# Turning the rows of h and y with a DMA transpose instead of with TensorE, in a two-layer graph kernel

## The chip, the core and the metric

The kernel runs on one core of a Trainium2 chip. The metric is the device time of one execution in microseconds (us). The engines work side by side, each on its own in-order list of instructions, and wait for each other by semaphores: TensorE (PE, with its weight loads shown apart as PEld), VectorE (DVE), ScalarE (ACT), GpSimd (POOL), and SyncE (SP), which here issues every DMA.

## What is computed

Shapes: `x` is 3125 x 256, there are 50,000 edges (`src`, `dst`), all weights are 256 wide.

```python
vals = 1 / deg(src)                                  # per row of the sum
def layer(x, W, b):                                  # used twice: W0, b0 and W1, b1
    neigh = segment_sum(vals * x[dst], src)
    return relu(concat([x, neigh]) @ W.T + b)
x = layernorm(x + layer(layer(x, W0, b0), W1, b1))
h_sparse = maxk(x @ W_neigh, 32)                     # only the 32 largest of each row stay
x = layernorm(x + x @ W_self + segment_sum(h_sparse[src], dst) / max(deg(dst), 1))
```

## The kernel before

The 3125 rows are cut into NT = 25 tiles of P = 125. First (up to about 183 us) the kernel builds the 25 x 25 blocks of the edge count matrix in SBUF (`ct`, `region[T]`), and stores a second copy of it in DRAM (`c_dram`) for the last part. A sum over neighbours is then a product with that matrix. All operands are float16 pairs, a high part and a low part side by side (`xs`, `a1`, `part`: 2 x 256 columns), so that one pass carries both.

**Layer 0** (`aggregate(0, T, ..)`, L1550 to L1560): 25 matmuls of 512 columns, one for each source tile ("blocks" below), sum tile T into one of three PSUM banks. DVE adds the halves, scaled, to `own_in` (`first_half` L901, `second_half` L906). ACT writes the high part of h, a relu, into `part[T % 2]` (`h_high` L1211), DVE the low part (L919). Then the 125 rows of `part` must be turned, because the next product wants the features on the partitions. PE does it with four matmuls against the identity into a PSUM bank (`turn` L1459 to L1462, called by `turn_h`), and ACT copies that to `tr_sb` (`tr_out` L1198 to L1202). `product(T)` (L1573) then multiplies `tr_sb` with the weights in six matmuls (`in_parts` L1455). ACT takes its two halves out (`own1_out` L1213: `own_st`, which SP stores, and the high part of `a1`), DVE makes the low part (`a1_low` L909).

Between these, DVE sums the count matrix of tile T + 2 (`sum_tree` L809) for the degrees, PE finishes them with two small matmuls (`degrees` L1584) and DVE inverts them (`invert` L888). ACT sums the other direction (`degree` L1221).

**Layer 1** does the same with `a1`: t2, then x is added and the rows normalised (L968 to L986), ACT writes the high part of y into `part` (L1277), POOL the low part (`y_low` L545), PE turns it (`turn_y`), `product(NT + T)` follows, and ACT takes out `hn` and `z_st` (`dense_out`). DVE picks the 32 largest of `hn` three tiles later (L936 to L953).

**The last part** is another 625 blocks (`last_sum` L1674), with the matrix loaded back from DRAM (`load_c` L408), and the second layernorm.

The order on every engine is written out by hand:

- PE, layer 0 (L1628 to L1654): from T = 5 on, 17 blocks of tile T, `turn_h(T - 1)`, 8 blocks, `degrees(T + 1)`, `product(T - 1)`. So a product runs one tile behind its sum.
- PE, crossing from layer 0 to 1 (L1657 to L1666): the blocks of tiles 0 and 1 of layer 1 are mixed with the turn and the product of the last tile, and with the waits for `a1_lo`.
- PE, layer 1 (L1667 to L1671): 12 blocks of tile T, `turn_y(T - 2)`, 13 blocks, `product(NT + T - 2)`.
- SP, layer 0 (L397 to L401): `load_own(0, T + 2)` (L375, waits for t2 of the tile before), `store_own1(T - 1)` (L385).
- SP, crossing (L418 to L429): two loads of x, the bias, `load_own(1, 0)` and `(1, 1)`, the last store, the weights.
- SP, layer 1 (L430 to L438): `load_own`, `load_x`, `store_z(T - 2)`, a wait for the sum of tile T, and `load_c(T - 1)` (763 KB).

Of the kernel before, what the change touches and what calls it, by code (L numbers as in the profile page):

```python
# [84 lines left out]
def gnn(nc, x, src, dst, w0, b0, w1, b1, wself, wneigh, out):  # L85
    ctx = ExitStack()
    with ctx:
# [131 lines left out]
        part = [lay(f"part{i}", [P, 2 * F], F16) for i in range(2)]  # L219
# [38 lines left out]
        tp = [bank[i][:, 0:4 * P].rearrange("p (c n) -> p c n", c=4) for i in (5, 6, 7)]  # L258
# [23 lines left out]
        slab_ready, tr_zeroed, eye_added, deg_summed = sem("slab_ready"), sem("tr_zeroed"), sem("eye_added"), sem("deg_summed")  # L282
# [14 lines left out]
        tp_done, tp_copied, mm_done = sem("tp_done"), sem("tp_copied"), sem("mm_done")  # L297
# [28 lines left out]
        def _(sp):  # L326
# [97 lines left out]
            load_bias(1, b1)  # L424
            load_own(1, 0)
# [35 lines left out]
        def _(pool):  # L461
# [71 lines left out]
            for t in tr_sb:  # L533
                nc.gpsimd.memset(t[:, :, P:128], 0.0).then_inc(tr_zeroed, 1)
# [7 lines left out]
            def y_low(T):  # L542
                pool.wait_ge(y_high, T + 1)
                out = part[T % 2]
# [21 lines left out]
        def _(dve):  # L566
# [348 lines left out]
            for T in range(NT):  # L915
# [3 lines left out]
                v.scalar_tensor_tensor(part[T % 2][:, F:2 * F], t2[T % 2][:, :], 0.0, part[T % 2][:, 0:F],  # L919
# [5 lines left out]
                if T:  # L925
                    a1_low(T - 1)
# [84 lines left out]
        def _(act):  # L1011
# [186 lines left out]
            def tr_out(i):  # L1198
                act.wait_ge(tp_done, i + 1)
                if i > 1:  # L1200
                    act.wait_ge(mm_done, i - 1)
                a.activation(tr_sb[i % 2][:, :, 0:P], tp[i % 2], ACT.Copy).then_inc(tp_copied, 1)  # L1202

            def part_free(i):
                if i > 1:
                    act.wait_ge(tp_done, i - 1)

            def h_high(T):
                act.wait_ge(t2_ready, T + 1)
                part_free(T)  # L1210
                a.activation(part[T % 2][:, 0:F], t2[T % 2][:, :], ACT.Relu).then_inc(hi_ready, 1)  # L1211
# [26 lines left out]
            for T in range(NT):  # L1238
                if T + 1 < NT:
                    degree(T + 1, 0)  # L1240
                if T == 1:
                    act.wait_ge(tr_zeroed, 2)
                if T:
                    tr_out(T - 1)
                if T == 0:
                    h_high(0)
# [7 lines left out]
                if T:  # L1254
                    own1_out(T - 1)
            tr_out(NT - 1)
# [17 lines left out]
            def y_high_part(T):  # L1274
                act.wait_ge(normed, T + 1)
                part_free(NT + T)
                a.activation(part[T % 2][:, 0:F], t2[(NT + T) % 2][:, :], ACT.Copy).then_inc(y_high, 1)  # L1277
# [5 lines left out]
            for T in range(NT):  # L1283
                if T > 1:
                    tr_out(NT + T - 2)
# [5 lines left out]
            tr_out(2 * NT - 2)  # L1291
            dense_out(NT - 2)
            sp_high_part(NT - 3)
            tr_out(2 * NT - 1)
# [10 lines left out]
        def _(pe):  # L1305
# [153 lines left out]
            def turn(out, parts, done):  # L1459
                for c in range(4):  # L1460
                    last = mm(out[:, c, :], parts[:, c * 128:(c + 1) * 128], ident16[:, 0:P], start=True, stop=True)  # L1461
                last.then_inc(done, 1)  # L1462

# [98 lines left out]
            def turn_h(T):  # L1562
                pe.wait_ge(lo_ready, T + 1)
                if T > 1:
                    pe.wait_ge(tp_copied, T - 1)
                turn(tp[T % 2], part[T % 2], tp_done)

            def turn_y(T):
                pe.wait_ge(y_ready, T + 1)
                pe.wait_ge(tp_copied, NT + T - 1)  # L1570
                turn(tp[(NT + T) % 2], part[T % 2], tp_done)

            def product(i):  # L1573

                pe.wait_ge(tp_copied, i + 1)
# [58 lines left out]
            aggregate(0, 3, 0, 9)  # L1634
            product(1)
            aggregate(0, 3, 9, 17)
            degrees(3)
            aggregate(0, 3, 17, NT)
            turn_h(2)
            aggregate(0, 4, 0, 9)  # L1640
            product(2)
            degrees(4)
            aggregate(0, 4, 9, 20)
            turn_h(3)
            aggregate(0, 4, 20, NT)
            degrees(5)
            product(3)
# [9 lines left out]
            pe.wait_ge(a1_lo, NT - 2)  # L1657
            aggregate(1, 0, 0, 11)
            turn_h(NT - 1)
            aggregate(1, 0, 11, 17)  # L1660
            product(NT - 1)
            aggregate(1, 0, 17, NT - 2)
            aggregate(1, 1, 0, 12)
            pe.wait_ge(a1_lo, NT)
            aggregate(1, 0, NT - 2, NT)
            aggregate(1, 1, 12, NT)  # L1666
# [23 lines left out]
            turn_y(NT - 2)  # L1690
# [3 lines left out]
            turn_y(NT - 1)  # L1694
# [5 lines left out]
            pe.wait_ge(tp_copied, 2 * NT)  # L1700
# [33 lines left out]
```

## Time and profile before

| what | value |
|---|---|
| time, three runs | 676.26, 677.28 and 681.02 us; median 677.28 us |
| the profiled execution | span 680.0 us from its first to its last instruction, on the one core; no other time of it is listed |
| mean granted TensorE clock | 0.984 of full speed |
| DMA | 73.09 MB, 107 GB/s on the average of the span |

The span of the profiled execution lies between the three times, 2.7 us above their median. Times in the rows below are microseconds from the span's start; a row of the timeline gives start, duration, engine, line, operation, output<-input, and in brackets how long the engine had been idle and what ended that. Layer 0 runs from about 183 to 363 us, layer 1 to 536 us, the last part to the end.

### The profile page before, as it was taken

The numbers are of one execution on the slowest core, as the hardware profiler recorded it, in microseconds if no ns is written. First come the engines' busy times: TensorE is split into PE (matmuls) and PEld (weight loads), VectorE is DVE, ScalarE is ACT, GpSimd is POOL, SyncE is SP. The second block draws the span as 40 slices with busy tenths as digits, with TensorE's granted clock in tenths as the row PEclk, the third lists the DMA queues.
The fourth block names the chain that finished last, engine by engine and source line by source line (L and its number), as shares of the span: only waits on it lengthen the run. The fifth ranks groups of instructions, "written<-read, shape, count | busy, mean of one in ns | idle before, by whom it ended". The sixth has DMA issues, their size and how long they took to land.

```text
span 680.0 us, 11272 instructions
## 1 busy us (share of the span) xinstructions
PE 650.4 (96%) x3982; PEld 337.4 (50%) x3983; DVE 496.9 (73%) x1274; ACT 338.8 (50%) x654; POOL 108.6 (16%) x187
## 2 busy tenths in 40 slices
PE   8788899999988999999999999999999999999996
PEld 3466566676534444444444444444444444444442
DVE  8898969999768788787882587878878855643333
ACT  3768779999768576767673233333333320000000
POOL 3001122222111001010110323222232210000000
PEclk9898979999999899999999999999999999999999
DMA  8643635555521111111112556565656423310000
GB/s 205 116 130 108 214 120 167 171 167 167 158 67 46 31 37 40 33 44 31 46 32 69 158 159 186 153 190 152 180 163 178 137 80 115 116 31 24 25 28 23
DMA packets 39543, 73.09 MB, mean 107 GB/s; under 512 B 3120, under 2 KB 32207, under 8 KB 39481
## 3 DMA queue, kind: packets, MB, share of 16 engines
q1 hardware_dynamic: 39481, 72.30, 35.8%
q8 instruction: 34, 0.56, 0.4%
q14 instruction: 28, 0.23, 0.1%
HBM read 38.91 MB, written 33.38 MB: 106 GB/s over the span
## 4 chain that ended last, share of the span: by engine, by line
PE 81%; DVE 10%; ACT 3%; DMA 2%; issue 2%; SPq 0%; POOL 0%; DVEq 0%; POOLq 0%; ACTq 0%
PE pair L1557 34%; PE bank L1681 10%; PE pair L1681 10%; PE bank L1481 6%; PE bank L1455 5%; PE bank L1447 4%; PE pair L1455 4%; PE pair L1367 4%; DVE hots L637 2%; PE bank L1461 1%; DVE tree L820 1%; DMA own_in<-own_dram 1%; DMA wparts_dram<-w_parts 1%; PE pair L1346 1%; PE bank L1467 1%
## 5 line engine op out<-in xcount | busy, mean ns | idle before, releaser
L1557 PE MATMUL pair<-xs,ct 125*128 125x512 f16 x625 | 143.7, 380 | 0.0
L1557 PE MATMUL pair<-a,ct 125*128 125x512 f16 x625 | 142.8, 379 | 0.0
L637 DVE TENSOR_TENSOR hots<-iota,jobs 125x1792 f16<-125x1792 f16 (+1 forms) x100 | 103.1, 1064 | 5.0 <-PE pair L1367 4.4
L1557 PEld LDWEIGHTS pair<-a,ct 125*128 125x128 f16 x625 | 61.1, 99 | 68.1
L1557 PEld LDWEIGHTS pair<-xs,ct 125*128 125x128 f16 x625 | 60.9, 100 | 67.6 <-issue 1.4
L1068 ACT ACTIVATE slab<-pair 125x875 f16<-125x875 f32 (+1 forms) x100 | 83.3, 854 | 13.2 <-PE pair L1367 8.6
L1226 ACT ACTIVATE a<-ct 125x1000 f16<-125x1000 f16 (+1 forms) x75 | 80.2, 1069 | 8.2 <-DMA c_dram<-slab 7.3
L1681 PE MATMUL bank<-xs,ct 125*128 125x512 f16 (+1 forms) x325 | 71.5, 379 | 0.0
L1681 PE MATMUL pair<-xs,ct 125*128 125x512 f16 x300 | 66.4, 379 | 0.0
L529 POOL TENSOR_TENSOR own_in<-own_in,bias_sb 125x256 f32<-125x256 f32 x50 | 38.2, 765 | 168.3 <-DMA own_in<-own_dram 168.2
L1301 ACT ACTIVATE sd<-mv,epsb 125x1 f32<-125x1 f32 x25 | 7.4, 294 | 113.9 <-DVE mv L1004 113.9
L1447 PEld LDWEIGHTS bank<-ident,slab 125*128 125x128 f16 x625 | 41.2, 100 | 39.8 <-issue 26.5
L901 DVE SCALAR_TENSOR_TENSOR t<-pair,rdeg,own_in 125x256 f32<-125x256 f32 x50 | 24.1, 483 | 50.3 <-PE pair L1557 46.9
L1447 PE MATMUL bank<-ident,slab 125*128 125x125 f16 x625 | 52.4, 223 | 6.3 <-DVE ct L791 3.0
L1367 PE MATMUL pair<-hots 125*128 125x125 f16 x625 | 52.8, 224 | 5.6 <-DVE hots L637 4.6
L1481 PE MATMUL bank<-w_t,x_t 128*125 128x512 f32 x100 | 56.0, 643 | 1.1 <-ACT x_t L1111 1.1
L1681 PEld LDWEIGHTS bank<-xs,ct 125*128 125x128 f16 (+1 forms) x325 | 32.3, 100 | 37.8
L1202 ACT ACTIVATE tr_sb<-bank 128x500 f16<-128x500 f32 x50 | 29.1, 581 | 42.3 <-PE bank L1461 42.3
L1367 PEld LDWEIGHTS pair<-hots 125*128 125x128 f16 x625 | 41.1, 100 | 11.6 <-issue 9.4
L1681 PEld LDWEIGHTS pair<-xs,ct 125*128 125x128 f16 x300 | 29.8, 99 | 34.4
L791 DVE COPY ct<-bank 125x1008 f16<-125x1008 f16 x50 | 33.6, 673 | 13.8 <-PE bank L1447 13.8
L820 DVE TENSOR_TENSOR tree<-tree,ct 125x630 uint16<-125x630 uint16 x75 | 37.3, 497 | 2.6
(205 smaller groups left out, 829.7 us busy)
## 6 DMA issues: line engine op xcount, KB each, us to landing
c_dram<-slab SPq DMA_DIRECT2D x25, 683.6 KB
ct<-c_dram SPq DMA_DIRECT2D x25, 683.6 KB
own_in<-own_dram SPq DMA_DIRECT2D x50, 125.0 KB
own_dram<-own SPq DMA_DIRECT2D x25, 125.0 KB
own_dram<-own_st SPq DMA_DIRECT2D x25, 125.0 KB
x_in<-in_x_dram SPq DMA_DIRECT2D x25, 125.0 KB
z_dram<-z_st SPq DMA_DIRECT2D x25, 125.0 KB
a<-z_dram SPq DMA_DIRECT2D x5, 625.0 KB
```

The costliest lines, as they stand in the source:

```text
L529: nc.gpsimd.tensor_tensor(own_in[k % 2][:, :], own_in[k % 2][:, :], bias_sb[:, :], ALU.add).then_inc(own_biased, 1)
L637: v.tensor_tensor(hots[k][:, :, :, :].rearrange("p w g (a d) -> p (w g) a d", d=2), iota, job, ALU.is_equal).then_inc(win_hot, 1)
L791: v.tensor_copy(ct[:, TG0[g]:TG0[g] + TG[g], t, :], tr16[1][0:P, 0:TG[g], 0:PC]).then_inc(tr_free[1], 1)
L820: step(v.tensor_tensor(tree[:, :], tree[:, :], quint[k], ALU.add))
L1068: a.activation(slab3[t % 2][:, :, lo * QW:hi * QW].rearrange("p b (w d) -> p b w d", d=QW), pair[f % 2][0:P, 0:n, 0:QKEY].rearrange("p w ( ...
L1226: a.activation(unread[:, 0:(hi - lo) * P].rearrange("p (b s) -> p b s", s=P), ct[:, lo:hi, T, 0:P], ACT.Copy, accum_out=deg_part[:, T, k:k ...
L1367: last = mm(pair[f % 2][:, u, 0:QKEY], hots[f][:, u, 0, :], hots[f][:, u, 1, 1:QKEY + 1], start=True, stop=True, skip_group_check=True)
L1447: last = nc.tensor.transpose(tr16[g % 2][:, i, 0:P], slab[par][:, (TG0[g] + i) * P:(TG0[g] + i) * P + 128], ident16[:, 0:P])
L1455: last = mm(out, lhs(2 * pt + h), w[:, h, q, :], start=h == 0 and k == 0, stop=h == 1 and k == 2, skip_group_check=True)
L1481: last = mm(bank[6][0:P, :].rearrange("p (a f) -> p a f", a=2), x_t32[:, h, :], w0_t[:, h::2, :], start=h == 0, stop=h == 1, skip_group_ch ...
L1557: ins = mm(agg[k % 3][0:lhs.shape[1], :], lhs, parts[l][:, t, :], start=t == 0, stop=t == NT - 1, skip_group_check=True)
L1681: ins = mm(out3[T % 8][0:lhs.shape[1], :], lhs, xs[:, b, :], start=b == 0, stop=b == NT - 1, skip_group_check=True)
```

## The change

The four turning matmuls, the bank they wrote and the ACT copy go. SP issues one DMA for each tile instead, `turn(i)`, which moves `part[i % 2]` (now 128 x 512, the lowest rows zeroed once) transposed to `tr_sb[i % 2]`. `product(i)` waits for that DMA (`turned`), and ACT waits for it before it overwrites `part`. To give the DMA room, in layer 0 every `product`, `own1_out`, `a1_low` and `store_own1` comes one tile later than before; in layer 1 the products keep their places. The zeroing of the padding moves from `tr_sb` to `part` and behind a wait.

```diff
+            def turn(i):                                      # on SP
+                sp.wait_ge(y_ready if i >= NT else lo_ready, i % NT + 1)
+                if i > 1:
+                    sp.wait_ge(mm_done, i - 1)
+                sp.dma_start_transpose(tr_sb[i % 2][:, :, :], part[i % 2][:, :]).then_inc(turned[i % 2], 16)
...
             for T in range(NT):                               # SP, layer 0
                 if T + 2 < NT:
                     load_own(0, T + 2)
-                if T:
-                    store_own1(T - 1)
+                turn(T)
+                if T > 1:
+                    store_own1(T - 2)
...
             load_bias(1, b1)                                  # SP, crossing
+            store_own1(NT - 2)
             load_own(1, 0)
...
             for T in range(NT):                               # SP, layer 1
+                if T:
+                    turn(NT + T - 1)
                 if T + 2 < NT:
                     load_own(1, T + 2)
...
+            turn(2 * NT - 1)
             store_z(NT - 2)
...
-            for t in tr_sb:                                   # POOL
-                nc.gpsimd.memset(t[:, :, P:128], 0.0).then_inc(tr_zeroed, 1)
+            pool.wait_ge(a0_split, NT + 2)
+            for i, t in enumerate(part):
+                nc.gpsimd.memset(t[96:128, :], 0.0).then_inc(part_zeroed, 1)
+                pool.wait_ge(part_zeroed, i + 1)
...
-                if T:                                         # DVE, layer 0; ACT's own1_out likewise
-                    a1_low(T - 1)
+                if T > 1:
+                    a1_low(T - 2)
+            a1_low(NT - 2)
             a1_low(NT - 1)
...
-            def tr_out(i):                                    # ACT; its calls go too
-                act.wait_ge(tp_done, i + 1)
-                if i > 1:
-                    act.wait_ge(mm_done, i - 1)
-                a.activation(tr_sb[i % 2][:, :, 0:P], tp[i % 2], ACT.Copy).then_inc(tp_copied, 1)
             def part_free(i):
                 if i > 1:
-                    act.wait_ge(tp_done, i - 1)
+                    act.wait_ge(turned[i % 2], 16 * (i // 2))
...
             def product(i):                                   # PE
-                pe.wait_ge(tp_copied, i + 1)
+                pe.wait_ge(turned[i % 2], 16 * (i // 2 + 1))
...
-            turn_h(0)                                         # PE, layer 0
             aggregate(0, 2, 9, 20)
-            product(0)
             degrees(2)
             aggregate(0, 2, 20, NT)
-            turn_h(1)
...
-            for T in range(5, NT):
-                aggregate(0, T, 0, 17)
-                turn_h(T - 1)
+            product(0)
+            for T in range(3, NT):
+                aggregate(0, T, 0, 8)
+                product(T - 2)
+                aggregate(0, T, 8, 17)
+                if T < 5:
+                    degrees(T)
                 aggregate(0, T, 17, NT)
-                if T + 1 < NT:
+                if 4 < T + 1 < NT:
                     degrees(T + 1)
-                product(T - 1)
...
+            pe.wait_ge(a1_lo, NT - 3)                         # PE, crossing
+            aggregate(1, 0, 0, 8)
+            product(NT - 2)
+            aggregate(1, 0, 8, NT - 3)
+            aggregate(1, 1, 0, 8)
             product(NT - 1)
+            pe.wait_ge(a1_lo, NT - 1)
+            aggregate(1, 0, NT - 3, NT - 1)
+            aggregate(1, 1, 8, NT - 1)
             pe.wait_ge(a1_lo, NT)
+            aggregate(1, 0, NT - 1, NT)
+            aggregate(1, 1, NT - 1, NT)
             for T in range(2, NT):                            # PE, layer 1
-                aggregate(1, T, 0, 12)
-                turn_y(T - 2)
-                aggregate(1, T, 12, NT)
+                aggregate(1, T, 0, NT)
                 product(NT + T - 2)
```

In the last part the two remaining turns (`turn_y(NT - 2)`, `turn_y(NT - 1)`) and the wait for the last copy go in the same way.

## Rows read from the trace of the kernel before

**Rows 1.** The page, part 4: shares of the chain that ended last, by engine.

```profile
PE 81%; DVE 10%; ACT 3%; DMA 2%; issue 2%; SPq 0%; POOL 0%; DVEq 0%; POOLq 0%; ACTq 0%
```

**Rows 2.** Busy time in stretches: length, busy us (instructions) of each engine, PEclk, DMA.

```profile
222.00:363.00 141.00, 141.00 (x737) 68.17 (x736) 110.21 (x311) 96.82 (x194) 14.54 (x19) 0.99 0.12 36
...
383.00:536.00 153.00, 153.00 (x775) 71.27 (x774) 119.47 (x430) 51.75 (x131) 42.94 (x65) 1.00 0.58 170
```

**Rows 3.** The chain in order of time, one tile of each layer: start, us, what.

```profile
301.60 3.67 PE pair L1557 x17
305.49 1.73 PE pair L1557 x8
307.28 1.32 PE bank L1455 x6
...
431.38 1.30 PE pair L1455 x6
432.68 2.59 PE pair L1557 x12
435.50 2.81 PE pair L1557 x13
```

**Rows 4.** Groups of instructions by line, the turning matmuls (busy us, mean ns | idle).

```profile
L1461 PE MATMUL bank<-ident,part 125*128 125x125 f16 x200 | 19.2, 218 | 1.7 <-issue 1.3 <-POOL part L545 0.4
```

**Rows 5.** The timeline, one tile of layer 0, from t2 to the low part of a1.

```profile
300.36 0.48 DVE L901 SCALAR_TENSOR_TENSOR t<-pair,rdeg,own_in 125x256 f32<-125x256 f32 x1 [0.48 <-PE pair L1557]
...
301.39 0.25 SPq L383 DMA_DIRECT2D own_in<-own_dram  x1
...
301.84 0.43 DVE L919 SCALAR_TENSOR_TENSOR part<-t,part 125x256 f16<-125x256 f32 x1 [0.48 <-ACT part L1211]
...
304.96 0.73 POOL L529 TENSOR_TENSOR own_in<-own_in,bias_sb 125x256 f32<-125x256 f32 x1 [6.30 <-DMA own_in<-own_dram]
...
306.43 0.48 DVE L911 SCALAR_TENSOR_TENSOR a<-pair,unscale,a 125x256 f16<-125x256 f32 x1
```

**Rows 6.** The timeline, one tile of layer 1, from t2 to the low part of y.

```profile
431.53 0.49 DVE L901 SCALAR_TENSOR_TENSOR t<-pair,rdeg,own_in 125x256 f32<-125x256 f32 x1 [1.32 <-PE pair L1557]
...
434.24 0.74 SPq L412 DMA_DIRECT2D ct<-c_dram  x2
...
437.33 0.67 POOL L545 TENSOR_TENSOR part<-t,part 125x256 f16<-125x256 f32 x1 [4.92 <-ACT part L1277]
```

**Rows 7.** The timeline, the first tiles of layer 0.

```profile
203.82 0.42 DVE L919 SCALAR_TENSOR_TENSOR part<-t,part 125x256 f16<-125x256 f32 x1 [0.81 <-ACT part L1211]
...
210.59 0.15 DVE L891 TENSOR_SCALAR rdeg<-bank 125x1 f32<-125x1 f32 x1
...
217.01 0.15 DVE L891 TENSOR_SCALAR rdeg<-bank 125x1 f32<-125x1 f32 x1
...
221.36 0.22 PE L1589 MATMUL bank<-ones,deg 125*125 125x1 f16 x1 [2.45 <-DVE deg L827]
```

**Rows 8.** Busy time in one of the stretches of 1 us behind that wait.

```profile
222.00:223.00 1.00, 1.00 (x3) 0.29 (x2) 0.58 (x2) 0.35 (x1) 0.00 (x0) 0.50 0.00 0
```

**Rows 9.** The chain in order of time: behind that wait, and the crossing between the layers.

```profile
221.64 2.43 PE bank L1455 x6
224.07 4.24 PE pair L1557 x17
...
363.18 1.31 PE bank L1455 x6
366.75 7.63 DMA own_in<-own_dram
...
382.98 1.30 PE bank L1455 x6
```

**Rows 10.** The timeline of the crossing: t2 and y of the first tile of layer 1.

```profile
375.33 0.48 DVE L901 SCALAR_TENSOR_TENSOR t<-pair,rdeg,own_in 125x256 f32<-125x256 f32 x1 [3.29 <-POOL own_in L529]
...
379.05 0.67 POOL L545 TENSOR_TENSOR part<-t,part 125x256 f16<-125x256 f32 x1 [2.79 <-ACT part L1277]
```

More of the change, by code:

```diff
@@ L218, in gnn @@
         t2 = [lay(f"t2_{i}", [P, F], F32) for i in range(2)]
-        part = [lay(f"part{i}", [P, 2 * F], F16) for i in range(2)]
+        part = [lay(f"part{i}", [128, 2 * F], F16) for i in range(2)]
         tr_sb = [lay(f"tr_sb{i}", [128, 4, 128], F16) for i in range(2)]
@@ L257, in gnn @@
         xp = bank[7][:, 0:2 * P].rearrange("p (c n) -> p c n", c=2)
-        tp = [bank[i][:, 0:4 * P].rearrange("p (c n) -> p c n", c=4) for i in (5, 6, 7)]
         agg, dense = bank[0:3], bank[3:5]
@@ L281, in gnn @@
         win_hot, win_done, win_read = sem("win_hot"), sem("win_done"), sem("win_read")
-        slab_ready, tr_zeroed, eye_added, deg_summed = sem("slab_ready"), sem("tr_zeroed"), sem("eye_added"), sem("deg_summed")
+        slab_ready, part_zeroed, eye_added, deg_summed = sem("slab_ready"), sem("part_zeroed"), sem("eye_added"), sem("deg_summed")
         tr_cleared = sem("tr_cleared")
@@ L296, in gnn @@
         hi_ready, lo_ready = sem("hi_ready"), sem("lo_ready")
-        tp_done, tp_copied, mm_done = sem("tp_done"), sem("tp_copied"), sem("mm_done")
+        turned, mm_done = [sem("turned0"), sem("turned1")], sem("mm_done")
         own1_copied, own1_stored, a1_hi, a1_lo = sem("own1_copied"), sem("own1_stored"), sem("a1_hi"), sem("a1_lo")
@@ L543, in y_low @@
                 pool.wait_ge(y_high, T + 1)
-                out = part[T % 2]
+                out = part[(NT + T) % 2][0:P, :]
                 nc.gpsimd.tensor_tensor(out[:, F:2 * F], t2[(NT + T) % 2][:, :], out[:, 0:F], ALU.subtract).then_inc(y_ready, 1)
@@ L918, in _ @@
                 dve.wait_ge(hi_ready, T + 1)
-                v.scalar_tensor_tensor(part[T % 2][:, F:2 * F], t2[T % 2][:, :], 0.0, part[T % 2][:, 0:F],
+                v.scalar_tensor_tensor(part[T % 2][0:P, F:2 * F], t2[T % 2][:, :], 0.0, part[T % 2][0:P, 0:F],
                                        ALU.max, ALU.subtract).then_inc(lo_ready, 1)
@@ L1210, in h_high @@
                 part_free(T)
-                a.activation(part[T % 2][:, 0:F], t2[T % 2][:, :], ACT.Relu).then_inc(hi_ready, 1)
+                a.activation(part[T % 2][0:P, 0:F], t2[T % 2][:, :], ACT.Relu).then_inc(hi_ready, 1)
             def own1_out(T):
@@ L1240, in _ @@
                     degree(T + 1, 0)
[L1241 to L1244, printed above, removed]
                 if T == 0:
+                    act.wait_ge(part_zeroed, 2)
                     h_high(0)
@@ L1253, in _ @@
                     act.wait_ge(deg_summed, NT * len(DG))
-                if T:
-                    own1_out(T - 1)
-            tr_out(NT - 1)
+                if T > 1:
+                    own1_out(T - 2)
+            own1_out(NT - 2)
             own1_out(NT - 1)
@@ L1276, in y_high_part @@
                 part_free(NT + T)
-                a.activation(part[T % 2][:, 0:F], t2[(NT + T) % 2][:, :], ACT.Copy).then_inc(y_high, 1)
+                a.activation(part[(NT + T) % 2][0:P, 0:F], t2[(NT + T) % 2][:, :], ACT.Copy).then_inc(y_high, 1)
             def sp_high_part(T):
@@ L1284, in _ @@
                 if T > 1:
-                    tr_out(NT + T - 2)
                     dense_out(T - 2)
@@ L1290, in _ @@
                     sp_high_part(T - 3)
-            tr_out(2 * NT - 2)
             dense_out(NT - 2)
             sp_high_part(NT - 3)
-            tr_out(2 * NT - 1)
             dense_out(NT - 1)
@@ L1457, in in_parts @@
                 return last
[L1459 to L1462, printed above, removed]
             def own_transposes(t, rows_):
@@ L1560, in aggregate @@
                     ins.then_inc(agg_done, 1)
[L1562 to L1571, printed above, removed]
             def product(i):
-                pe.wait_ge(tp_copied, i + 1)
+                pe.wait_ge(turned[i % 2], 16 * (i // 2 + 1))
                 if 1 < i < NT + 2:
@@ L1689, in _ @@
             last_sum(0, 0, 20)
-            turn_y(NT - 2)
             last_sum(1, 0, 8)
@@ L1693, in _ @@
             last_sum(1, 8, 20)
-            turn_y(NT - 1)
             pe.wait_ge(t2_ready, 2 * NT)
@@ L1699, in _ @@
             last_sum(3, 0, 20)
-            pe.wait_ge(tp_copied, 2 * NT)
             last_sum(4, 0, 20)
```

22 lines of the change are left out of this document (removed).

## Prediction

> **What bounds the kernel now.** I began with the shares of the chain that ended last: PE is 81% of it and ACT, where the removed copy ran, 3% [rows 1]. That is an average, so the next view is busy time by stage: through most of layer 0 and all of layer 1 PE is busy without a gap, 141.00 of 141.00 us and 153.00 of 153.00 us, while DVE has 110 and 119, ACT 97 and 52 [rows 2]. In these stages PE's work alone sets the pace, and what PE no longer does is gained as long as nothing makes it wait. The chain in order of time then gives the pace of a tile [rows 3]. Layer 0: 17 blocks 3.67 us, a gap to the next piece of 305.49 - 305.27 = 0.22 us, 8 blocks 1.73, degrees 0.06, product 1.32: 7.00 us. Layer 1: 1.30 + 2.59 + 0.23 + 2.81 = 6.93 us. A block is 3.67 / 17 = 0.216 us.
>
> The gap is the turn. Its rows have a mean of 218 ns for 200 matmuls and 19.2 us busy [rows 4], and the reader could take 19.2 us for the price. But matmuls overlap, so their durations hold latency that the next one covers. What a turn takes from the pace is the 0.22 us.
>
> **The change part by part.**
>
> *Removed on PE.* Fifty turns of 0.22 us are 11.0 us, 1.6% of the span, and this is the most the change can bring. ACT's 50 copies go too; ACT is off the chain in both layers, so they are worth nothing.
>
> *Does another engine become the bound?* Without the turn, PE's tile is 6.78 us in layer 0 and 6.70 in layer 1. DVE's own tile in layer 0 runs from 300.36 to 306.43 + 0.48 = 306.91, so 6.55 us with the idle 0.48 before it left out [rows 5]. It stays under 6.78, by only 0.23 us. In layer 1 DVE sits idle 1.32 us of every 6.9 [rows 6], which leaves 5.6. PE stays the bound and keeps the whole 0.22.
>
> *Added: one transposing DMA for each tile.* Call D the time from the moment its input is ready to the moment PE may start the product. No row shows such a DMA, nor any from SBUF to SBUF. The nearest row by size (125 KB against 128 KB) is the load of `own_in`: issued at 301.39, used by POOL at 304.96, 3.57 us [rows 5]. The longest of its kind, with other loads ahead of it in the queue, took 7.63 us [rows 9]. From below the bound is the issue alone, 0.25 us [rows 5]. I take 3.5 us, next to the nearest row, for in layer 0 the DMA engines are 12% busy [rows 2] and little lies ahead in the queue.
>
> *What hides D.* Layer 0: the sum of a tile ends 307.28 - 7.00 - 0.06 = 300.22, its low part at 301.84 + 0.43 = 302.27, 2.05 us later [rows 3, 5]. Its product now comes a whole tile and 8 blocks behind, 6.78 + 0.06 + 1.73 = 8.57 us after that sum. Cover: 6.5 us. Layer 1: the sum ends at 431.38, POOL ends y at 438.00, 6.62 us later [rows 3, 6]; the product stands two tiles behind, 13.40 us. Cover: 6.8 us. The 763 KB of `load_c`, issued at 434.24, go ahead in the same queue and have 3.8 us until then [rows 6]; the engines are 58% busy [rows 2], so most of that has passed. With D = 3.5 both steady states lose nothing.
>
> *What queues behind the new waits on SP.* In layer 0 it is `store_own1`, which has more than a tile's time. In layer 1 it is `load_own`, `load_x`, `store_z` and `load_c`; the turn is issued 6.62 us after a sum, and the next of these waits for t2 of the following tile, about 8.0 us after. So SP loses nothing if the issue takes up to 1.4 us; an issue here takes 0.25 [rows 5]. If it takes longer, `load_own` comes later, and it is used a tile afterwards.
>
> *The first tiles of layer 0.* Here DVE sets the pace: its `invert` of tiles 3 and 4 are 6.42 us apart, and PE sits idle 2.45 us at `degrees(5)` [rows 7]. The four turns saved up to there are worth nothing. Worse, PE has `product(1)` ahead of `degrees(3)`, on which DVE waits. The low part of tile 1 is ready at 204.24 [rows 7]; + 3.5 is 207.74; + product 1.30 + 9 blocks 1.94 is 210.98, so `invert(3)` starts some 0.5 us behind its 210.59. PE reaches `degrees(4)` another 25 blocks and a product later, 6.70 us, at 217.7, 0.8 us behind 217.01. That passes on to `degrees(5)`: +0.8 us.
>
> *Layer 0 from tile 5.* Twenty turns (4 to 23) at 0.22: -4.4 us.
>
> *The crossing.* Count from the end of the last sum of layer 0, now 363.18, called A. PE's new order: 8 blocks, product, 22 blocks, product, 18 blocks, 2 blocks: 50 x 0.216 + 2 x 1.32 = 13.44 us until both first sums of layer 1 are done, then 25 blocks to `product(NT)` at A + 18.8. `load_own(1, 0)` is now issued 3.57 us after A and lands 7.63 later [rows 9]. In the new order it follows a store that waits for product 23, at some A + 4.0, so its bias is added by about A + 12.4. In time. So t2 starts at A + 13.4, y follows 379.72 - 375.33 = 4.39 later [rows 10], at A + 17.8, plus D is A + 21.3. PE waits 2.5 us for the first turned y, with nothing else it may do. Today that product starts at 382.98 - 363.18 = 19.8 [rows 9], so the crossing gets 1.5 us longer though it holds two turns less.
>
> *What that wait costs besides.* After the idle 2.45 us at 221.36 [rows 7] the granted clock was 0.50, the lower level of 1.2 GHz [rows 8], and the next product took 2.43 us and the next 17 blocks 4.24, against 1.32 and 3.67 at 2.4 GHz [rows 3, 9]: 1.7 us lost. A wait of 2.5 us is the same size, so I add 1.7.
>
> *Layer 1 and after.* Twenty-four turns (y 1 to 24): -5.3 us. The last y has more than the 6.8 us of cover, since 20 blocks of the last part come in between.
>
> *At nothing.* POOL's larger memsets and their wait lie in a stretch in which POOL then waits for the bias. With that cover gone they would cost their own length, under 1 us, once. `a1_low` and `own1_out` are moved by a tile, not added.
>
> **The sum.** 0.8 - 4.4 + 1.5 + 1.7 - 5.3 = -5.7 us on the span of 680.0, which is -0.84%. On the median of 677.28 that is 671.6 us. In D the sum moves by 2 us for each us: once in the first tiles, once in the crossing.
>
> **The rivals.**
>
> *A quicker DMA, nearly the whole gain.* With D = 2.5 the first tiles lose nothing and the crossing waits 1.5 us. Waits of that size are not among the rows that show a fall of the clock, so the 1.7 goes: -4.4 + 0.5 - 5.3 = -9.2, 668.1 us. For it: both ends are in SBUF, and a round trip to DRAM, which the 3.57 us hold, falls away. Against it: turning is more than copying, and no row shows its speed.
>
> *A middling DMA, nearly nothing gained.* With D = 5.5, about the middle between 3.57 and 7.63, the sum is -5.7 + 2 x 2.0 = -1.7, 675.6 us. The mechanism is that the four groups of 128 columns are turned one behind the other, while each copying row above is one stream. The Trainium skill ("VectorE: DVE Perf Modes", section on the three transpose paths) speaks against the change here: it gives 1309 ns for a 128 x 128 block by DMA and 390 ns on TensorE. Four blocks in a row would by that page be an estimated 5.2 us, and the sum -2.3. For TensorE the trace disagrees with it in this place: four blocks take 0.22 us from the pace [rows 3].
>
> *Slower: the DMA outlasts its cover.* Up to D = 6.4 the sum stays below zero. Beyond 6.5 PE waits at every product of layer 0, and its tile becomes 2.05 + D - 1.79 = D + 0.26. At D = 7.0 that is 7.26 instead of 7.00: 20 x 0.26 = +5.2; first tiles 0.8 + 3.5 = 4.3; crossing 1.5 + 3.5 + 1.7 = 6.7; layer 1 at (6.62 + 7.0) / 2 = 6.81 instead of 6.93: -2.9. Sum +13.3, 690.5 us. For it: such waits have been 7.63 us here [rows 9]. Against: only with other loads ahead.
>
> *The change does nothing to the pace.* If DVE's tile in layer 0 grows by the 0.23 us that it has left, layer 0 keeps 6.99 and its 4.4 us are lost; the sum is -1.3, 676.0. The four engines' in-order waits were read from one tile, so this can't be excluded.
>
> **How the numbers follow.** Chances: forecast 0.40, quicker 0.24, middling 0.13, slower 0.18, DVE in the way 0.05. A change of 1% (6.8 us) is about what a measurement of this kernel tells from none. The quicker case lies beyond it, and of the forecast's own spread, 669 to 674.5 us (D from 3.0 without the fall of the clock to 5.0), some quarter does: faster 0.34. Slower by over 1% is the slower case: 0.18. The rest, 0.48, is within 1%. The range is 667.0 to 684.0: below, the quicker case with a little to spare; above, the slower case up to D of some 6.6, which leaves about 0.15 of the chance out there.
>
> **What would show it.** Right: the chain has 7.00 -> 6.78 and 6.93 -> 6.70 us for a tile, PE waits for `turned` at `product(NT)` alone, some 2.5 us, with a granted clock of 0.50 behind it, and `degrees(3)` comes later than now. Wrong: PE waits before every product (D above 6.5), DVE without idle time before t2 in layer 0, or the rows of SP showing an issue of several us, which would move `load_c` and `load_own` too. The single number that decides is D.

## The result, and the profile after

The changed kernel takes 692.96 us (median of 4 runs, 692.39 to 699.1) against 679.15 us for the kernel before (4 runs). The quotient of these two medians is 1.0203; the ratio on record, which isn't formed from them, is 1.0237, with a 95% interval of 1.0178 to 1.0295. So it is slower; the interval leaves open whether by more than 2%. The forecast was 671.6 us and its range ended at 684.0. The profiled execution took 692.39 us, with a span of 690.6 us.

First the page, part 4, of the changed kernel: shares of the chain that ended last, by engine and (first entries) by line. It answers to [rows 1].

```profile
PE 58%; DMA 17%; DVE 11%; SPq 6%; ACT 5%; issue 3%; POOL 0%; DVEq 0%; ACTq 0%
```

PE fell from 81% to 58%; the DMA, 2% before, has 17%, and SP's own queue 6%. Next the busy time in the two layers, as in [rows 2].

```profile
222.00:357.00 135.00, 135.00 (x656) 63.24 (x655) 108.97 (x306) 85.23 (x171) 14.36 (x19) 1.00 0.26 57
383.00:545.00 162.00, 145.36 (x657) 63.20 (x655) 116.13 (x420) 38.98 (x105) 42.52 (x63) 1.00 1.16 169
```

In layer 0 PE is still busy without a gap. In layer 1 it is idle for 16.6 of 162 us, and the DMA's share went from 0.58 to 1.16 although it moves the same 169 GB/s (170 before). A share above 1 can't be work: transfers that wait are counted as busy.

The chain in order of time gives the tile of layer 0, to set beside [rows 3]:

```profile
295.32 1.75 PE pair L1554 x8
297.07 1.30 PE pair L1457 x6
298.37 3.67 PE pair L1554 x17
302.04 0.00 PE bank L1575
302.04 0.06 PE bank L1576
```

From 295.32 to 302.10 it is 6.78 us, as forecast. In layer 1 the chain no longer runs on PE. One round of it:

```profile
413.89 8.56 DMA tr_sb<-part
...
422.49 1.48 PE bank L1457 x6
...
424.00 0.47 ACT hn L1269
424.47 0.37 ACT z_st L1272
...
424.86 1.03 SPq L423
...
426.00 1.32 SPq L419
...
427.37 1.19 SPq L419
...
428.65 8.88 DMA tr_sb<-part
```

This is a closed loop through SP's in-order list: the turn lands, the product runs, ACT takes it out, SP stores z (L423), issues the two parts of `load_c` (L419), and only then issues the turn of the tile after next. A round takes 428.65 - 413.89 = 14.76 us for two tiles. PE's timeline over one of these tiles shows what is left for it:

```profile
414.98 1.47 PE L1457 MATMUL pair<-w_lay,tr_sb 128*128 128x512 f16 x6 [1.07 <-DMA tr_sb<-part]
416.28 5.56 PE L1554 MATMUL pair<-a,ct 125*128 125x512 f16 x25
422.49 1.47 PE L1457 MATMUL bank<-w_lay,tr_sb 128*128 128x512 f16 x6 [0.65 <-DMA tr_sb<-part]
```

Before every product PE waits for the turn, and a tile is 422.49 - 414.98 = 7.51 us (median of the layer 7.59) instead of 6.91. The turn's own rows, in layer 0 and then in layer 1 (duration is the issue on SP; below it the time from issue to landing):

```profile
L389 SPq DMA_TRANSPOSE tr_sb<-part x25: 1189/1191/1298, 193.5 to 358.3; - x25
DMA to landing us min/median/max: 2.4/3.0/4.4
...
L389 SPq DMA_TRANSPOSE tr_sb<-part x25: 1194/1278/2172, 374.9 to 551.7; - x25
DMA to landing us min/median/max: 2.4/9.0/10.0
```

The same transfer takes 3.0 us in one layer and 9.0 in the other. By stages, each measured from the first matmul named to the next (degrees(T) is the pair of small matmuls; the build of the count matrix ends where the first block of layer 0 starts):

| stage | before, us | after, us | difference | forecast |
|---|---|---|---|---|
| build of the count matrix | 183.46 | 179.11 | -4.4 | 0 |
| first block to degrees(5) | 37.91 | 39.69 | +1.8 | +0.8 |
| degrees(5) to degrees(24) | 134.66 | 130.51 | -4.2 | -4.4 |
| degrees(24) to the first product of layer 1 | 26.79 | 28.08 | +1.3 | +1.5, and +1.7 for the clock |
| from there to the first block of the last part | 153.42 | 169.76 | +16.3 | -4.8 (22 turns) |
| the rest | 143.77 | 143.41 | -0.4 | -0.4 (2 turns) |

The build is not touched by the change; in the profiles below it lies between 179.1 and 183.7 us without any order, so it is left out of every comparison. The other five rows add up to +14.8 us, near the 13.8 between the two medians; the forecast's own sum was -5.7. One stage holds the whole surprise.

### The profile page after: what moved, and what is told of

Its sections match the earlier page's. It is cut to its first block, busy times and chain, and to the rows that moved or that the text cites. A ratio compares the mean times of both kernels' runs of the same rounds, so it can differ in the third digit from the quotient of the medians.

```text
span 690.6 us, 10824 instructions
## 1 busy us (share of the span) xinstructions
PE 639.2 (93%) x3782; PEld 323.4 (47%) x3783; DVE 498.3 (72%) x1274; ACT 314.0 (45%) x604; POOL 110.7 (16%) x187
## 4 chain that ended last, share of the span: by engine, by line
PE 58%; DMA 17%; DVE 11%; SPq 6%; ACT 5%; issue 3%; POOL 0%; DVEq 0%; ACTq 0%
PE pair L1554 17%; DMA tr_sb<-part 15%; PE bank L1652 10%; PE pair L1652 9%; PE bank L1478 5%; PE bank L1457 5%; SPq L419 4%; PE bank L1449 4%; DVE hots L650 3%; PE pair L1369 3%; PE pair L1457 2%; SPq L423 2%; DVE ct L804 1%; DMA own_dram<-own_st 1%; DMA wparts_dram<-w_parts 1%
## 5 line engine op out<-in xcount | busy, mean ns | idle before, releaser
L1554 PE MATMUL pair<-a,ct 125*128 125x512 f16 x625 | 139.0, 379 | 0.0
L1449 PEld LDWEIGHTS bank<-ident,slab 125*128 125x128 f16 x625 | 40.3, 99 | 39.3 <-issue 25.8
L1478 PE MATMUL bank<-w_t,x_t 128*125 128x512 f32 x100 | 54.2, 624 | 1.2 <-ACT x_t L1125 1.2
L1457 PE MATMUL bank<-w_lay,tr_sb 128*128 128x512 f16 x150 | 37.1, 384 | 12.0 <-DMA tr_sb<-part 12.0
L1457 PE MATMUL pair<-w_lay,tr_sb 128*128 128x512 f16 x150 | 36.6, 380 | 9.6 <-DMA tr_sb<-part 8.2
```

The source lines that it names most:

```text
L1449: last = nc.tensor.transpose(tr16[g % 2][:, i, 0:P], slab[par][:, (TG0[g] + i) * P:(TG0[g] + i) * P + 128], ident16[:, 0:P])
L1457: last = mm(out, lhs(2 * pt + h), w[:, h, q, :], start=h == 0 and k == 0, stop=h == 1 and k == 2, skip_group_check=True)
L1478: last = mm(bank[6][0:P, :].rearrange("p (a f) -> p a f", a=2), x_t32[:, h, :], w0_t[:, h::2, :], start=h == 0, stop=h == 1, skip_group_ch ...
L1554: ins = mm(agg[k % 3][0:lhs.shape[1], :], lhs, parts[l][:, t, :], start=t == 0, stop=t == NT - 1, skip_group_check=True)
```

## The experiments

All variants are of the changed kernel unless said. "Land" is the time from issue to landing of the turns of layer 1 (min/median/max). The times of the kernel before that go with them were 679.15 us (changed kernel), 677.48 (e1 to e4), 676.65 (e5 to e8) and 680.07 (e9 to e11); the three groups of variants ran on three different chips, so between groups the ratios are to be compared, and the stages of the profiles.

| run | time, us (runs) | ratio to before, 95% interval | land, us | tile of layer 1, us |
|---|---|---|---|---|
| changed kernel | 692.96 (4) | 1.0237 [1.0178, 1.0295] | 2.4/9.0/10.0 | 7.59 |
| e1_no_c | 673.55 (1) | one run | 2.4/2.5/4.8 | 6.69 |
| e2_turn_first | 676.86 (10) | 0.9992 [0.9969, 1.0014] | 2.4/6.6/8.3 | 6.70 |
| e3_split | 672.47 (10) | 0.9933 [0.9909, 0.9958] | 2.4/3.9/5.2 | 6.69 |
| e4_l1_on_pe | 678.83 (10) | 1.0024 [1.0000, 1.0048] | none | 6.91 |
| e5_split_order | 670.75 (11) | 0.9901 [0.9868, 0.9935] | 2.4/4.0/5.6 | 6.69 |
| e6_split_order_first | 665.59 (4) | 0.9818 [0.9777, 0.9860] | 2.4/2.5/4.6 | 6.69 |
| e7_before_split | 677.14 (10) | 0.9992 [0.9966, 1.0017] | none | 6.91 |
| e8_act_queue | 694.89 (4) | 1.0258 [1.0208, 1.0308] | 2.4/5.9/10.3 | 6.70 |
| e9_split_loads | 672.90 (9) | 0.9908 [0.9883, 0.9933] | 2.4/3.6/7.0 | 6.69 |
| e10_split_z | 674.90 (7) | 0.9947 [0.9914, 0.9980] | 2.4/6.3/9.4 | 6.73 |
| e11_order_no_split | 674.03 (10) | 0.9934 [0.9907, 0.9960] | 2.4/7.2/8.3 | 6.75 |

**Is it the traffic of `load_c`?** In e1_no_c only one of 25 column blocks of each matrix row is loaded, except for the last tile:

```diff
+                    n = N if T == NT - 1 else P
-                    sp.dma_start(region[home(T)][lo:hi, 0:N], c_dram[T, lo:hi, :]).then_inc(c_loaded[T % CR], 16)
+                    sp.dma_start(region[home(T)][lo:hi, 0:n], c_dram[T, lo:hi, 0:n]).then_inc(c_loaded[T % CR], 16)
```

> Left out: the 763 KB load of the matrix for each tile of layer 1 is cut to 125 of its 3125 columns (30 KB); the order on every engine stays. All three theories put the loss of layer 1 (169.9 us from the first product of y to the last part, against 153.4 before) on the DMA queue, and so expect a tile of 6.70 us, a turning DMA of at most 4 us from issue to landing instead of some 9, and 693 - 21 = about 672 us. If the turning DMA itself, SP's in-order waits or PE's new place of the product were at fault, the tile would stay near 7.5 us and the time near 690.

Measured: the turn lands in 2.5 us, the tile is 6.69 us, PE waits for a turn 2.8 us in all, nearly all of it in the crossing, and the time is 673.55 us. So without the bytes of `load_c` the turn isn't late, although the 125-row transfers still go beside it; by itself it needs 2.4 to 2.5 us even in layer 1. What in that traffic delays it, its place ahead of the turn or the engines that it shares, this run can't tell.

**Its place in the queue.** In e2_turn_first `load_c` is issued right behind the turn and no longer ahead of the next one:

```diff
                 if T:
                     turn(NT + T - 1)
+                if T > 1:
+                    sp.wait_ge(agg_done, NT + T)
+                    load_c(T - 2)
...
-                if T:
-                    sp.wait_ge(agg_done, NT + T + 1)
-                    load_c(T - 1)
```

> Layer 1's load of the matrix is issued right behind the turning DMA of the same round and not right ahead of the next one; same transfers, same bytes. Theory A (place in the queue: the turn waits behind 763 KB): the turn finds the queue nearly empty, lands in 3.5 to 4.5 us, tile 6.70 us, about 672 us. Theory B (five of the 16 DMA engines carry all the transfers of 125 rows besides their share of the rest, take longer than a tile for it, and the turn, which needs all 16, ends with them): the load of these five is the same, so the tile stays above 7.3 us and the time at 685 to 693 us.

Measured: 676.86 us, tile 6.70 with single ones up to 7.7, PE waits 5.7 us in all. The loop through SP is cut and 16 us come back. But the turn still takes 6.6 us, just at its cover of 6.8, with the `load_c` ahead of it issued a whole tile earlier. Both theories missed part of it: A had the turn landing in 3.5 to 4.5 us, B had the tile above 7.3 us and the time above 685. Place explains the size of the loss, not why a transfer that needs 2.5 us takes 6.6.

**The five engines.** The packet records of the trace (not one of the views) hint at another cause. In layer 1 the kernel before has 757 end-of-transfer packets of 4 bytes in 120 us, 44 for each tile of 6.93 us. `load_c` is issued as 112 + 13 rows; its two parts can make 16 + 13, and the three transfers of 125 rows (`own_in`, `x_in`, z) 5 each: together 44. This fits the Trainium skill ("DMA: Bandwidth & Descriptors", section on why a DMA increments its semaphore by 16): a transfer is spread over the largest number of engines up to 16 that divides its rows, and the lowest-numbered ones are taken; for 125 that is five, the same five each time. The trace agrees in the count, 44; which engines they are its packet records don't say. How many they are, the records do show: from 400 to 520 us, in the changed kernel as in the kernel before, never more than six of the 1 KB packets of these transfers are in flight together, on the average of a quarter of a microsecond. From 406.5 to 408.5 us in the changed kernel, for instance, it is 5.4 of them, with 11.2 of the 6250-byte packets of `load_c` beside them. The turn has 512 packets of 256 bytes; in e1_no_c, where it is alone, 16 to 18 are in flight together. The end of one turn (issued at 405.69) in the changed kernel, packets that took over 2 us:

```
start us  ns    bytes   end us
409.12    5020   256    414.14
409.13    5015   256    414.15
409.14    5022   256    414.16
409.15    5007     4    414.16
409.75    4398   256    414.15
409.76    4391     4    414.15
409.76    4389     4    414.15
409.76    4388     4    414.15
409.76    4387     4    414.15
409.84    4308     4    414.15
409.84    4306     4    414.15
```

Eleven packets, which is 16 less five, reach the end of their share at 409 to 410 and stay there until 414.15, all to the same moment. Meanwhile the records show five others at work: from 409.9 to 410.8 us 5.4 packets of 1 KB are in flight and none of `load_c`, from 411.0 to 412.5 us 5.0 packets of `load_c` and none of 1 KB. That reads as eleven engines held by the turn until the other five have done their 125-row transfers, then their share of `load_c`, and then their share of the turn. In e3_split these three transfers of layer 1 go in 112 + 13 rows as well:

```diff
-                sp.dma_start(z_dram[T], z_st[T % 2][:, :]).then_inc(z_stored[T % 2], 16)
+                for lo, hi in PARTS:
+                    sp.dma_start(z_dram[T, lo:hi], z_st[T % 2][lo:hi, :]).then_inc(z_stored[T % 2], 16)
```

and in the same way for `own_in` and `x_in`, with the counts of their waits doubled.

> In layer 1 each transfer of 125 rows (own_in, x_in, z) is issued in two pieces of 112 and 13 rows, as the matrix already is, so that 16 engines share it; the order, the bytes and the place of the turn behind the 763 KB stay. Theory B (five overloaded engines): their 75 packets of 1 KB become some 24 on each engine, the turn lands in 4 to 5 us, tile 6.70 us, about 672 us. Theory A (place in the queue): the turn still waits behind the 763 KB, the tile stays above 7.3 us and the time above 685 us. Against both: if the three more issues on SP (some 0.75 us a tile) delay the rest, the tile is 6.8 to 7.0.

Measured: the turn lands in 3.9 us, with `load_c` ahead of it as in the changed kernel; the tile is 6.69 us; 672.47 us. This is what theory B said, and theory A's tile above 7.3 us is out. In the packet records up to 17.6 packets of 1 KB are in flight together now. Busy time over the same 120 us of layer 1 (length, busy us of PE, PEld, DVE, ACT, POOL, PEclk, DMA share, GB/s), first of the changed kernel:

```profile
400.00:520.00 120.00, 107.45 (x487) 46.91 (x486) 87.31 (x318) 29.01 (x79) 31.11 (x46) 1.00 1.16 170
```

and of e3_split:

```profile
400.00:520.00 120.00, 120.00 (x558) 54.86 (x557) 99.04 (x359) 33.88 (x90) 35.67 (x54) 1.00 0.88 195
```

More bytes a second in a smaller share: in the changed kernel much of the share was engines held and not at work. Of its 1.16, the packets of 256 and of 4 bytes make 0.56, of the 0.88 of e3_split 0.23, although a turn is the same 512 packets in both. The advice of the same page of the Trainium skill (its rules for kernel authors) not to make two transfers of disjoint halves of the partitions, since both spread over the same 16 engines, doesn't hold for 125 rows here, which don't: the ratio to the kernel before is 0.9933 with the split and 1.0237 without.

Does each of the three count? e9_split_loads splits only `own_in` and `x_in`, e10_split_z only the store of z.

> Of the three 125-row transfers of layer 1 only the two loads (own_in, x_in) go in 112 + 13 rows; the store of z stays whole. Theory A (the work of the five engines adds up, whatever direction it has): between the changed kernel (9.0 us to land, 692) and the full split (3.9 us, 672.5), two thirds of the way: the turn lands in 5 to 6.5 us, tile of layer 1 6.70, 673 to 676. Rival (the store of z, which stands right behind the turn or ahead of the next one, is what holds it): the turn stays above its cover of 6.8 us and the time above 685.

> The counterpart: only the store of z goes in 112 + 13 rows, the two loads stay whole. Theory A (the work adds up): one third of the way, the turn lands in 6.5 to 8 us, at or above its cover, tile of layer 1 6.7 to 7.2 us, 676 to 686. Rival (the store alone holds it): it lands in about 4 us, 673.

Measured: two transfers split, 3.6 us to land and 672.90 us; one split, 6.3 us and 674.90. The landing time falls as transfers are taken off the five: 9.0 us with none split, 6.3 with one, 3.6 with two; the third brings nothing more (3.9). So both rivals, which put all on the store of z, are wrong in the landing times, and theory A is right in direction only: in each of the two runs the turn landed sooner than it said, and the two gains, 2.7 and 5.4 us, are together more than the 5.1 of the whole split. The stretch from degrees(24) to the last part takes 197.84 us in the changed kernel, 179.29 in e10_split_z, 177.14 in e9_split_loads and 176.69 in e3_split: as soon as the turn lands within its 6.8 us in the median, nearly all is back.

Is the split a gain by itself? e7_before_split makes it in the kernel before.

> The kernel before, with only the three transfers of layer 1 cut into 112 + 13 rows. Theory A (PE sets the pace at 6.91 us a tile there, and the DMA's unevenness is hidden): ratio 1.000 within 0.3%, layer 1 at 6.9 us a tile. Rival (the split gains by itself, whatever turns the rows): ratio near 0.993, as with the split on the changed kernel.

Measured: 0.9992 [0.9966, 1.0017], tile 6.91 us. It is not: in the kernel before, the same uneven engines were hidden. Its end packets rise from 44 to 116 for each tile, which is 4 x (16 + 13).

**Another queue.** In e8_act_queue the turns of layer 1 are issued by ACT on its own queue:

```diff
-                if T:                                         # SP, layer 1
-                    turn(NT + T - 1)
...
+                turn(NT + T)                                  # ACT, behind y_high_part(T)
```

> The changed kernel, with the turns of layer 1 issued from ACT's own queue, so that they don't stand behind the other transfers in SP's queue. Theory A (a turn waits for its place in SP's queue): it lands in under 5 us, tile of layer 1 at 6.70 us, about 673. Theory B (a turn is done only when the five loaded engines have done their share, and those are busy with the 125-row transfers whichever queue it comes from): it lands in 5 to 8 us, tile between 6.7 and 7.3, 673 to 685. If the tile stays above 7.3 us, the queue has no part in it.

Measured: theory B in the landing times, wrong in the total. From the third turn on it lands in 3.4 to 4.6 us, then later and later, up to 9.8 us at the 19th, and in 5.9 us in the median. So a queue of its own doesn't keep it from being late; that it is the loaded engines again fits, but no run splits the transfers beside this queue. The total of 694.89 us has two causes. From the first product of layer 1 to the last part it takes 158.08 us against 148.70 in e3_split, and 6.3 us of the difference are waits for five of the later turns. The rest no theory had: the first turn of the layer took 10.27 us while PE had nothing else, and then the product and the 25 blocks took 2.74 and 6.39 us, against 1.30 and 5.40 in the steady tiles, as behind the fall of the clock in [rows 9]; here too the granted clock was 0.50 from 390 to 394 us. The stretch from degrees(24) to the first product grew by 8 us, to 36.02. In the chain in order of time:

```profile
379.26 10.27 DMA tr_sb<-part
389.58 2.74 PE bank L1464 x6
392.32 6.39 PE pair L1561 x25
```

Why this one took 10.27 us is not settled.

**Layer 0 alone.** e4_l1_on_pe turns the rows of layer 1 on PE again:

```diff
-                aggregate(1, T, 0, NT)
+                aggregate(1, T, 0, 12)
+                turn_y(T - 2)
+                aggregate(1, T, 12, NT)
```

> Only layer 0 is turned by DMA; layer 1 has its four matmuls and the ACT copy back, at their old places. Theories A and B alike: the loss of layer 1 goes, its tile is 6.93 us as before, layer 0 keeps 6.78 us, the crossing has no wait for the first y. From 693: -21.6 + 5.3 - 2 = about 675 us, 0.3 to 0.6% below the kernel before. A rival: layer 0's gain is an artefact of the single profile, then the time equals the kernel before within 0.2%.

Measured: 678.83 us, 1.0024 [1.0000, 1.0048], so the 675 us missed. The rival's time comes near, but not for its reason: the 4.1 us of layer 0 are there, and most of them are given back in the first tiles (39.40 us, +1.5) and in the crossing (28.77 us, +2.0), where PE now waits 2.8 us for POOL's low part of the first y.

**The two smaller losses.** e5_split_order adds two moves to e3_split:

```diff
+                if T == 2:                                    # DVE, ahead of sum_tree(4)
+                    a1_low(0)
...
-            for T in range(2, NT):                            # PE, layer 1
+            aggregate(1, 2, 0, NT)
+            aggregate(1, 3, 0, 12)
+            product(NT)
+            aggregate(1, 3, 12, NT)
+            product(NT + 1)
+            for T in range(4, NT):
```

> The three transfers of layer 1 in 112 + 13 rows, and besides two moves in the order: DVE makes the first low part of a1 ahead of a sum tree instead of behind it, and PE puts the first product of layer 1 after 12 blocks of tile 3 of layer 1 instead of ahead of them. Theory A (the lost time of the first tiles is PE's wait for that low part, and that of the crossing PE's wait for the first turned y): 672.5 - 1.4 - 2.3 = about 669, ratio 0.987; the first block to degrees(5) takes about 38 us instead of 39.7, and PE has no wait for a turn in the crossing. Rival (the first tiles are set by DVE's sum trees, and the crossing by what follows from the first y, so both only move the wait): 672 to 673, ratio as with the split alone.

Measured: 670.75 us, between the two. The first move does what theory A said: 37.83 us to degrees(5) instead of 39.3. Another 1.7 us, which no theory had, come from the clock, which in this profile doesn't fall behind degrees(5) (last section). The second only moves the wait: `product(NT)` no longer waits, `product(NT + 1)` does, 2.3 us, because the second turn stands behind the first `load_c`. From degrees(24) to the last part e3_split and e5_split_order both take 176.69 us. So the rival is right for the crossing. e6_split_order_first puts `load_c` behind the turn as well:

> As the kernel before it in this list, and the load of the matrix is issued right behind the turn instead of ahead of the next. Theory A (once the five engines are relieved, the place in the queue is worth little): the turn lands in about 3 us instead of 3.9 in layer 1, PE waits for neither, and the time is the same within 0.3%. Rival (the place in the queue still decides part of it): faster by over 0.5%.

Measured: 665.59 us, 0.9818 [0.9777, 0.9860]. The turn lands in 2.5 us, PE waits for turns 0.4 us in all, and the same stretch takes 174.31 us, 2.4 less, which is the 2.3 us wait that is gone. The medians lie 5.2 us apart, which would be the rival's, but the profiles show only those 2.4. The rest goes with the clock: the five runs of e5_split_order with a mean granted clock of 0.992 or more took 666.83 to 668.01 us, the six with less 670.75 to 676.49, and all four of e6_split_order_first had 0.992 or more, at 665.16 to 666.32. Between like clocks it is some 2 us, 0.3%, as theory A said, so the two theories aren't told apart. The page, part 4, of this run:

```profile
PE 83%; DVE 9%; ACT 3%; DMA 2%; issue 2%; SPq 0%; DVEq 0%; ACTq 0%
```

It is the fastest version of this study and the one in which PE is rid of the turns and hardly waits for them; but not all of its gain is the turn's, as the earlier `a1_low(0)` and the clock are in it too. e11_order_no_split is the same without the split:

> The fastest version so far without its split: the two moves in the order and the load of the matrix right behind the turn, with the 125-row transfers whole. Theory A (the split is needed as soon as the turn is to land in time, since otherwise the five engines are late): the turn lands in 6 to 7 us as in the kernel with the load moved alone, PE waits some 5 us in all, time about 676.5 - 3 = 673.5, ratio 0.993 to 0.997. Rival (the place of the load and the order alone do it, the split is worth nothing beside them): 666, ratio near 0.982.

Measured: 674.03 us, as theory A said; the turn lands in 7.2 us in the median and PE waits 4.5 us in all. With the order right but the five engines loaded the turn just misses its cover; the split is needed beside the order.

## Why the prediction was wrong, step by step

**The step that failed** is the one on what hides D, in its second half: "The 763 KB of `load_c` ... go ahead in the same queue and have 3.8 us until then; the engines are 58% busy, so most of that has passed. With D = 3.5 both steady states lose nothing." The 58% is a mean over 16 engines. The turn needs all 16 at once and ends with the last, and the mean says nothing of the five that carry the 125-row transfers. The kernel before could have shown it: from 400 to 520 us its packets of 1 KB take 3.2 engines' time and those of `load_c` 5.9. If five engines carry all of the first and 40 rows in 125 of the second (7 of the 112 and one of the 13 each), that is an estimated 3.2 + 1.9 = 5.1 engines' time on five, so no time to spare, packets that wait counted in. D was 3.0 us in layer 0, close to the 3.5 taken, and 9.0 in layer 1, against a cover of 6.8.

With D known, the rest follows from the forecast's own rows and SP's delay. From the end of a sum to its product the DMA side takes 6.62 us until y is ready [rows 3, 6], some 0.5 until SP issues the turn (0.83, 0.51 and 0.20 in three tiles), and 9.0 to land: 16.1. On PE the same way holds two products and two sums, 2 x 6.70 = 13.4, and three waits. So a wait is (16.1 - 13.4) / 3 = 0.9 us and the tile 7.6; measured 7.59. The rival's formula, (6.62 + D) / 2, left the third wait out. Over the 22 tiles of the stage 0.9 us make 19.8 of the 21.1 us that lie between the +16.3 measured and the -4.8 forecast; the mean tile, (169.76 - 1.30) / 22 = 7.66 us with the longer first ones, makes all of it.

The upper end of the range has a slip of its own: by the rival's formulas 684.0 us belong to a D of 6.8 us, not of 6.6.

**The slower rival** had the right mechanism, a DMA that outlasts its cover, and the right condition ("only with other loads ahead"), but it was priced in layer 0, where few loads are ahead, and taken as harmless in layer 1, where they are. Its 18% was too little for a quantity that no row showed.

**The issue on SP** was taken as 0.25 us from a row of another kind of DMA; it is 1.19 in layer 0 and 1.28 in layer 1 in the median, with single ones of up to 2.17. "Harmless up to 1.4" looked at that instruction alone. What was missed is that the turn closes a loop on SP: behind late turns the issues of `load_c` grew from 388 to 1180 ns in the median and those of z from 341 to 1036, and all stand ahead of the next turn.

**Layer 0 from tile 5**: right. Tile 6.78 us, -4.2 against -4.4; DVE has 0.23 us of idle time left ahead of t2, as worked out.

**The first tiles**: right in sign, +1.8 against +0.8, but by another wait. The turn came sooner than thought (D 3.0), and `invert(3)` was not late. PE's timeline shows where it was lost:

```profile
202.59 1.47 PE L1457 MATMUL bank<-w_lay,tr_sb 128*128 128x512 f16 x6 [0.43 <-DMA tr_sb<-part]
...
210.95 1.46 PE L1457 MATMUL pair<-w_lay,tr_sb 128*128 128x512 f16 x6 [1.41 <-issue]
```

`product(1)` waits 0.43 us for its turn; `product(2)` waits 1.41 us, for which the view names no releaser. DVE's timeline does:

```profile
210.37 0.48 DVE L924 SCALAR_TENSOR_TENSOR a<-pair,unscale,a 125x256 f16<-125x256 f32 x1
```

This is `a1_low(0)`, done at 210.85, which `product(2)` waits for (L1563) and which DVE does behind the whole `sum_tree(4)`. The forecast took moved instructions as free; this one was moved behind 4 us of other work. e5_split_order confirms it: with `a1_low(0)` ahead of the sum tree `product(2)` has no such wait.

**The crossing**: right in the sum, by luck. The forecast had the first product of layer 1 at A + 21.3 after a wait of 2.5 us; A is 356.10 now:

```profile
377.40 1.47 PE L1457 MATMUL bank<-w_lay,tr_sb 128*128 128x512 f16 x6 [2.36 <-DMA tr_sb<-part]
```

377.40 - 356.10 = 21.3. But two terms in it were off, and cancel:

```profile
370.51 0.48 DVE L914 SCALAR_TENSOR_TENSOR t<-pair,rdeg,own_in 125x256 f32<-125x256 f32 x1
...
374.23 0.67 POOL L558 TENSOR_TENSOR part<-t,part 125x256 f16<-125x256 f32 x1 [3.79 <-ACT part L1282]
...
374.92 1.20 SPq L389 DMA_TRANSPOSE tr_sb<-part  x1
```

t2 starts at A + 14.4 and not at 13.4, since DVE has `a1_low(NT - 1)` and the degrees of the other direction ahead of it, so y is ready at A + 18.8 and not at 17.8; and D is 2.5 us here and not 3.5. The granted clock stayed at 1.00 behind this wait, so the added 1.7 us was wrong.

**The middling rival** had four groups of 128 columns turned one behind the other. The whole turn, issued with nothing in the way, landed in 2.4 to 2.5 us, so four groups in a row, if that is how it goes, don't take this rival's 5.5 us. The Trainium skill ("VectorE: DVE Perf Modes", section on the three transpose paths) gives 1309 ns for one block of 128 x 128; four of them in a row would be an estimated 5.2 us, and the trace doesn't agree with adding them up.

## What to carry to other kernels

Before work is put on a shared resource, look at its most loaded part and not at its mean: a transfer that uses all DMA engines lands with the slowest of them, and a row count such as 125 loads five. When a transfer replaces compute, follow what stands ahead of it and behind it on the issuing engine's list for two rounds, since a late landing can delay the issue of the next one. And an instruction that is "only moved" has to be checked against what it now stands behind.

## What was not expected of the hardware

The DMA transpose of 128 x 512 float16 from SBUF to SBUF took 1.19 us to issue on SP, against 0.25 for a plain DMA of nearly the same size (125 KB), and 2.4 us to land when nothing stood in its way; it was 512 packets of 256 bytes.

The clock after an idle PE was not decided by the length of the wait alone. In the kernel before, 2.45 us idle ahead of degrees(5) was followed by a granted clock of 0.50 [rows 8]. In e7_before_split, with the same order on PE, the same wait was not; its timeline shows the wait:

```profile
219.17 0.22 PE L1593 MATMUL bank<-ones,deg 125*125 125x1 f16 x1 [2.45 <-DVE deg L831]
```

and the busy time of a stretch behind it a granted clock of 1.00:

```profile
220.00:221.00 1.00, 1.00 (x6) 0.45 (x5) 0.52 (x2) 0.54 (x2) 0.00 (x0) 1.00 0.00 0
```

From degrees(5) to degrees(24) that is 132.98 us against 134.66, the 1.7 us of the forecast. In the family of the changed kernel the same stretch took 130.5 us in the changed kernel and the seven variants without the earlier `a1_low(0)`, and 128.83 in the three that have it (e5, e6 and e11), though their wait at degrees(5) is 2.6 us too. In that family the fall goes along with what PE did some microseconds before, a wait of 1.4 us ahead of `product(2)` (at 210.95 in the changed kernel); between the kernel before and e7_before_split there is no such difference. A rule can't be drawn from these runs.
